# First queries and keys placed by 0/1 products, values projected by rows, and smaller first loads in a decoder kernel

## The reference

```python
# step 1: self attention, 8 sequences of 128 tokens, 8 heads of 8
qk = (x @ Wqk_w.T + Wqk_b).reshape(b, n, H, E, 2)
q, k = qk[..., 0], qk[..., 1]                      # (b, H, n, 8)
v = (x @ Wv_w.T + Wv_b).reshape(b, n, H, E)
attn = softmax(q @ k^T) / 8
x = layernorm(x + (attn @ v) @ Wo_w.T + Wo_b)
# step 2: cross attention of the context with x, softmax over 128 rows
x = layernorm(x + softmax(ctx @ x^T * 128**-0.5) @ ctx)
# step 3: linear layer with routed low-rank part
# step 4: 4-bit coded weights: attention products, gate, up, down
# step 5: cross attention with keys Wk, queries Wq and biases bq, bk
# step 6: gated feed-forward net with ternary weights
```

## Time and profile before

| | us |
|---|---|
| median of three runs | 661.75 (661.51 to 661.8) |
| the profiled execution | 661.55 |
| its span, first to last instruction | 659.7 |
| PE busy | 642.2 (97%), 3232 records |
| DVE busy | 394.1 (60%) |
| ACT busy | 384.2 (58%) |
| mean granted clock of PE | 0.996 |

### The profile page before, as it was taken

One profiled execution on the slowest core, in us unless ns is written; L12 is line 12 of the kernel. 1 busy time (PEld: TensorE's weight loads), 2 busy tenths in 40 slices (PEclk: granted clock), 3 DMA queues, 4 the chain that ended last, 5 costly groups with the idle time before them and its releaser, 6 DMA issues.

```text
span 659.7 us, 8518 instructions
## 1 busy us (share of the span) xinstructions
PE 642.2 (97%) x3232; PEld 473.7 (72%) x3232; DVE 394.1 (60%) x622; ACT 384.2 (58%) x528; POOL 67.5 (10%) x117
## 2 busy tenths in 40 slices
PE   9999999999999999999999999999999999999995
PEld 6655455554547778888888888886777888888874
DVE  2778867749688859676766527324675221215566
ACT  3877778866787777766767236213456333226532
POOL 1122213302231000000000000001111000000012
PEclk9999989999999999999999999999999999999999
DMA  6870287522323324332421003038000222100002
GB/s 226 294 269 33 85 267 192 160 80 64 100 99 108 103 70 141 102 108 77 126 79 31 1 0 129 1 113 365 0 5 29 80 97 67 61 1 0 1 32 97
DMA packets 25015, 64.19 MB, mean 97 GB/s; under 512 B 5478, under 2 KB 10022, under 8 KB 24079
## 3 DMA queue, kind: packets, MB, share of 16 engines
q1 hardware_dynamic: 23486, 61.50, 28.9%
q10 hardware_dynamic: 1488, 2.15, 1.0%
HBM read 58.90 MB, written 4.73 MB: 96 GB/s over the span
## 4 chain that ended last, share of the span: by engine, by line
PE 88%; DVE 4%; ACT 4%; issue 2%; POOL 1%; POOLq 0%; ACTq 0%; DVEq 0%
PE bank L1004 19%; PE bank L1083 8%; PE bank L1082 8%; PE bank L991 7%; PE bank L992 7%; PE bank L993 7%; PE bank L766 4%; PE bank L843 4%; PE bank L597 3%; PE bank L716 2%; PE bank L679 1%; PE bank L690 1%; PE bank L631 1%; PE bank L622 1%; PE bank L751 1%
## 5 line engine op out<-in xcount | busy, mean ns | idle before, releaser
L1191 ACT ACTIVATE line<-line 128x1024 f32<-128x1024 f32 x87 | 91.2, 1049 | 0.1
L991 PE MATMUL bank<-xh,wh 128*128 128x512 f32 x224 | 87.5, 391 | 0.0
L992 PE MATMUL bank<-xl,wh 128*128 128x512 f32 x224 | 87.4, 390 | 0.0
L993 PE MATMUL bank<-xh,wl 128*128 128x512 f32 x224 | 87.3, 390 | 0.0
L1004 PE MATMUL bank<-wh,xh 128*128 128x512 f32 x192 | 76.0, 396 | 0.2 <-DVE xl L2082 0.2
L1004 PE MATMUL bank<-wh,xl 128*128 128x512 f32 x192 | 74.9, 390 | 0.0
L2165 DVE SCALAR_TENSOR_TENSOR arena<-bank,ff_s,arena 128x512 f32<-128x512 f32 x28 | 21.0, 751 | 72.9 <-PE bank L1083 63.7
L2082 DVE TENSOR_TENSOR xl<-arena,xh 128x1024 fp32r<-128x1024 f32 (+1 forms) x26 | 29.6, 1141 | 35.2 <-ACT xh L1508 35.0
L1082 PE MATMUL bank<-xh,wh 128*128 128x512 f32 x128 | 50.2, 392 | 0.0
L1083 PE MATMUL bank<-xl,wh 128*128 128x512 f32 x128 | 49.9, 390 | 0.0
L1508 ACT ACTIVATE xh<-arena 128x1024 fp32r<-128x1024 f32 (+1 forms) x26 | 25.6, 991 | 41.3 <-PE bank L1004 34.8
(11 more groups left out here) (211 smaller groups left out, 1276.2 us busy)
## 6 DMA issues: line engine op xcount, KB each, us to landing
codes<-in_c_gu SPq DMA_DIRECT2D x14, 512.0 KB, 3.6
scales<-in_s_gu SPq DMA_DIRECT2D x28, 256.0 KB, 3.8
codes<-in_t_gu SPq DMA_DIRECT2D x8, 512.0 KB, 4.2
codes<-in_c_dn SPq DMA_DIRECT2D x7, 512.0 KB, 5.1
scales<-in_s_dn SPq DMA_DIRECT2D x14, 256.0 KB, 4.0
fold<-in_t_dn SPq DMA_DIRECT2D x1, 3584.0 KB, 16.6
scales<-in_t_gu SPq DMA_DIRECT2D x6, 512.0 KB, 3.7
x<-in_x SPq DMA_DIRECT2D x2, 1024.0 KB, 6.0
```

The source lines that it names most:

```text
L991: pe.matmul(dst, wh[:, s, c:c + P], xh[:, k, cols], start=(k == 0), stop=False)
L992: pe.matmul(dst, wh[:, s, c:c + P], xl[:, k, cols], start=False, stop=False)
L993: last = pe.matmul(dst, wl[:, s, c:c + P], xh[:, k, cols], start=False, stop=(k == KD - 1))
L1191: nc.scalar.activation(below(slot), below(slot), ACT.Prelu, bias=bias, scale=scale, alpha=alpha).then_inc(bent, 1)
```

## The change

1. **Placement.** Queries and keys of the first 256 tokens no longer go over DRAM. A table `places` of zeros and ones is made from the identity by DVE; PE multiplies it with the projected rows (`place_heads`, four products of 256 columns into banks 2 and 3), DVE copies the queries and ACT the keys (`keys_placed`) to their places. The other three quarters still go over DRAM. The constant row is now row 8 of each group of 32 instead of row 0.
2. **Values by rows.** `v_projection`, its ACT copy and the transposes `v_rows` are gone. `values(b)` multiplies the tokens (as weights) with Wv's 64 columns, four products per block, so that the result has tokens on partitions; DVE adds the bias while it copies (`v_out`). `keep_warm` is gone; `values(4)` to `values(7)` stand near its places.
3. **First loads.** The weights are split in a q/k part (256 KB) and a v part (128 KB); the first quarter of x transposed is split in two halves of 128 tokens (256 KB each). ACT's queue starts with three transfers ahead of its first instruction; the first 512 KB of x hold two blocks instead of four. The warm-up has four products instead of six.
4. **Order of the fillers.** `key_span` is moved by one: three key steps in t = 1, one in t = 7. Therefore the second key step of an iteration is the first of a group, and ACT's `key_group_out` is moved ahead of `heads_exp`. The decoding units run one iteration later in the loop (seven in place of eight) and the extra unit is put in step 4 of the second phase. `key_columns` is cut in four pieces, each ahead of one of the four products of `keys(0)`.

```diff
-WARM = 6
-PLAN = ([1] * NT, [2], [0] + [1] * NT, [1] * 3 + [2, 2] + [1] * 5)
+WARM = 4
+PLAN = ([0] + [1] * (NT - 1), [2], [0, 1, 1, 1, 2] + [1] * 4, [1] * 3 + [2, 2] + [1] * 5)
...
-    first = 2 + KD * (t - 2)
+    first = 3 + KD * (t - 2)
...
         @block.sync
-            sp.dma_start(qkvT, i["qkvT"]).then_inc(in_qk, 16)
+            sp.dma_start(qkT, i["qkT"]).then_inc(in_qk, 16)
+            sp.dma_start(xT[:, :, P:PC], i["xT"][:, :, P:PC]).then_inc(in_x0b, 16)
...
-            project_in(0)
             sp.dma_start(qk_b[:, :], i["qk_b"]).then_inc(in_pb, 16)
-            sp.dma_start(v_b[:, :], i["v_b"]).then_inc(in_pb, 16)
-            project_in(1)
-            sp.wait_ge(q_blank, 1)
-            sp.wait_ge(k_blank, 1)
-            rows_to_dram(0)
-            dram_to_heads(0)
+            sp.dma_start(wv, i["wv"]).then_inc(in_wv, 16)
+            sp.dma_start(v_b, i["v_b"].partition_broadcast(P)).then_inc(in_pb, 16)
+            project_in(2)
+            sp.dma_start(codes[:, 0, :], i["c_qkv"][0]).then_inc(in_codes[0], 16)
+            sp.dma_start(s_qkv[:, :], i["s_qkv"]).then_inc(in_sqkv, 16)
+            sp.wait_ge(blanked, 1)
             rows_to_dram(1)
...
+            def values(b):
+                if b == 0:
+                    pe.wait_ge(in_wv, 16)
+                elif b == 4:
+                    pe.wait_ge(v_ready, 1)
                 for k in range(KD):
+                    last = pe.matmul(bank[V_BANK][:, b % 4 * HA:(b % 4 + 1) * HA], xT[:, k, b * P:(b + 1) * P], wv[:, k, :], start=(k == 0), stop=(k == KD - 1))
...
+            def place_heads():
+                pe.wait_ge(blanked, 1)
+                pe.wait_ge(qk_ready, 1)
+                for w, dst in enumerate((q_place, k_place)):
+                    for g in range(HG):
+                        last = pe.matmul(dst[:, g * PC:(g + 1) * PC], places[:, HG * w + g, :], qk_st[:, 0:PC], start=True, stop=True)
+                    last.then_inc(place_ps, 1)
...
+            def key_columns(c):
+                if c == 0:
+                    pe.wait_ge(kw_ready, KD + 2)
+                for m in range(3 * c, min(3 * c + 3, 2 * KD)):
+                    n, e = divmod(m, KD)
+                    pe.matmul(bank[0][:, m:m + 1], folded[:, n, e * P:(e + 1) * P], picked[:, :], start=True, stop=True)
...
             def keys(n):
                 for c in range(KD):
+                    if n == 0:
+                        key_columns(c)
                     last = pe.matmul(turn_bank(n)[:, :], kq_w[:, c, e * P:(e + 1) * P], ctxT[:, g, c, :], start=(c == 0), stop=(c == KD - 1))
...
         @block.scalar
             for t in range(2, NT):
-                unit_bends(t, 0)
+                unit_bends(t - 1, 0)
                 x_T_out(t - 2)
+                key_group_out(t - 2)
                 heads_exp(t)
-                key_group_out(t - 2)
-                unit_bends(t, 1)
+                unit_bends(t - 1, 1)
                 norm_tail(t - 1)
...
         @block.vector
-            for t in range(NT):
+            for t in range(1, NT):
                 augment(t)
-                if t < 2:
+                if t == 1:
+                    unit_part(0, 0)
+                    v_out(1)
+                else:
+                    if t == 2:
+                        unit_part(1, 0)
+                    unit_part(t - 1, 1)
+                attention_norm(t - 1)
...
```

More of the change, by code:

```diff
@@ L634, in v_rows @@
[L634 to L644 removed]
+                for h in range(2) if n == 0 else (0,):
+                    size = P if n == 0 else PC
+                    if h:
+                        pe.wait_ge(in_x0b, 16)
+                    t = slice(n * PC + h * P, n * PC + h * P + size)
+                    for k in range(KD):
+                        last = pe.matmul(bank[QK_BANK[n]][:, h * P:h * P + size], qkT[:, k, :], xT[:, k, t], start=(k == 0), stop=(k == KD - 1))
@@ L777, in _ @@
             warm_up()
-            for n in range(2):
-                qk_projection(n)
-                v_projection(n)
-            qk_projection(2)
-            pe.wait_ge(ident_ready, 1)
-            v_rows(0)
-            scores(0)
-            v_projection(2)
-            max_rows(0)
+            qk_projection(0)
+            values(0)
+            values(1)
+            place_heads()
+            qk_projection(1)
+            scores(0)
+            values(2)
+            values(3)
+            pe.wait_ge(ident_ready, 1)
+            max_rows(0)
+            qk_projection(2)
+            scores_T(0)
             qk_projection(3)
-            scores_T(0)
-            v_projection(3)
             heads_out(0)
             scores(1)
-            keep_warm(6)
+            values(4)
+            values(5)
             for t in range(1, NT):
@@ L1878, in _ @@
             sims_prob(1)
-            unit_part(NT + 1, 1)
+            unit_part(NT, 1)
             for u in plan(2, 1):
```

191 lines of the change are left out of this document (86 added, 105 removed).

## The result

The changed kernel takes 668.24 us (median of 4 runs, 667.65 to 669.8) against 661.77 of the kernel before on the same chip: 1.0103 times as long, with a 95% interval of 1.0081 to 1.0124. It is slower by 1%, where 660.0 was predicted, and it lies above the predicted range. Ratios leave out any execution more than 1.5% above the fastest of its kernel, here one of 1660.4 among four of the kernel before; its other three took 661.51 to 661.8. The profiled execution took 668.24 with a span of 666.3, so 6.6 us more span than the 659.7 of before.

What follows compares the result with a forecast made beforehand. PE's stream was taken to bound the kernel. Terms -2.2 + 1.8 - 1.8 + 0.5 = -1.7 took the profiled 661.55 to 659.85; with the median 0.2 above, 660.0 us, range 657.9 to 662.2.

Steps and rivals of the forecast that it cites:

- Term 1: Opening, to block 2's row maxima: earlier first scores put PE ahead, -2.2 us (range -0.8 to -3.3).
- the opening stays at half clock: Rival for the opening: PE does less, clock stays at or falls to 1.2 GHz until about 13; 663.5 us, chance 0.12.
- Term 2: Loop: key copy ahead of the exponential delays head products 0.3 us in iterations 2 to 7, +1.8 us.
- the loop absorbs the copy: Rival for the loop: a gap or slack takes the key copy, cost 0 or near it; 658.2 us, chance 0.15.
- Term 3: Bias columns at keys(0): spread between large products, the half clock should not come, -1.8 us.
- the first rival: At keys(0): the clock falls all the same despite the spread columns; 661.8 us, chance 0.16.
- Term 4: Second phase: ACT's extra bends in step 4 make PE wait for prob before context(5), +0.5 us.

Runs made afterwards that it cites:

- e12: e9 with Wv ahead of the q/k bias, and x's third and fourth quarters and the codes held back until Wv landed: 659.5 us, ratio 0.9977.
- e3: Changed kernel with six products of zeros between the first projection and the first values: 664.83 us, ratio 1.0074.
- e0: Changed kernel unedited, measured again: 666.17 us, ratio 1.007.
- e4: Changed kernel with the key steps' order of before and the key group's copy behind the exponential again: 661.05 us, ratio 1.0017.
- e6: e5 with the key steps' order of before and the key copy behind the exponential again: 663.67 us, ratio 1.0031.
- e8: Changed kernel with keep_warm's 6 and 5 identity products put back ahead of values(4) and values(6): 666.65 us, ratio 1.0099.
- e10: e9 with keep_warm's identity products put back and a warm-up of six products: 662.27 us, ratio 1.0036.
- e1: Changed kernel with the q/k bias issued behind Wv and the value bias in SP's queue: 664.32 us, ratio 1.008.
- e5: Changed kernel with Wv and both biases moved to ACT's queue behind 256 KB of x, x's second quarter to SP's: 666.46 us, ratio 1.0114.
- e9: e6 with a semaphore for each bias and the q/k bias ahead of Wv in ACT's queue: 660.57 us, ratio 1.0013.
- e2: Changed kernel with x's second and fourth quarters issued only once the first half quarters are there: 664.26 us, ratio 1.0041.
- e11: Kernel before with only the new key-step order and the key copy ahead of the exponential: 666.25 us, ratio 1.0086.
- e7: Kernel before with only the bias columns spread between the four products of keys(0): 660.0 us, ratio 0.9985.
- e13: e12 with the extra decoding unit in the second phase's last step in place of step 4: 658.79 us, ratio 0.9973.

## Why the prediction was wrong

**Term 1, the opening: -2.2 predicted, +4.0 measured. This is the step that failed.** The sentence was "Values of two blocks wait for Wv, third in its queue, until about 7.0". Wv stands fourth there, behind the q/k bias, and the landing times were those of the kernel before, where two transfers followed one another on SP's queue and ACT issued its first at 5.45; in the changed kernel ACT's three, 1.25 MB, are issued from 0.73 on. Wv landed at 10.0. Two costs came with it: the values started 2.76 later than in e12, and the clock fell behind the wait, which took 1.74 at the values (3.47 to the placing, in e12 1.73) and 1.66 at the placing (3.45 to the next projection, in e12 1.79). Together they are the 6.16 by which the first scores differ. ACT's late first copy (its biases at 11.4) lay beside the values. The rival "the opening stays at half clock" described this, named the wait for Wv as a cause, and got a chance of 0.12; it priced 7 us at half clock with 3.5, and the clock was low from 10.05 until beyond 16, for 3.4; the wait of PE itself it did not price. That filling PE's wait keeps the clock up is shown by e3, for its profiled execution. It is not the length of the wait alone: the clock fell behind waits of 1.66 to 2.88 in six profiled executions (the changed kernel, e0, e4, e6, e8, e10), not behind 0.83 to 1.27 (e1, e5, e9), and not behind 3.14 in e2. All the rest of the walk was right: in e12, with Wv there in time, first scores stand at 12.63 (12.6 predicted), the row maxima of block 2 at 32.15 (32.1), and before them is the wait for DVE that made up the sum. So the mechanism and the size of the gain were right, and its condition, a load in time, was not met.

The Trainium skill ("DMA: Bandwidth & Descriptors", Anatomy of one DMA) gives a fit, for one transfer on the GpSimd path, of some 2.0 us plus the bytes at 436 GB/s, which for 128 KB is an estimate of 2.3 us. The traces here, on SP's and ACT's queues, show 7.5 with 1.25 MB beside it, 3.9 and 4.5 with less: in a loaded opening the fit does not give the landing, and the measurement decides.

**Term 2, the loop: +1.8 predicted, +2.4 measured.** The wait of PE was forecast at 0.5 and is 0.52. The period grew by 0.44 in the iteration shown and not by 0.3; interval by interval, from the maxima of block 2 to `sims(0)`, it is 0.65, 0.42, 0.44, 0.34, 0.24 and 0.29. Of the first, 0.2 is there in e12 too, with the order of before. The exponential starts 0.47 behind the key copy, and the key copy 0.50 behind the copy of the transposed block (42.06, 41.59, 41.09). Before, the exponential began 0.69 behind that copy, because it waited for the scores. So ACT's row moves by 0.28, as forecast. But the head products moved by 0.43, since PE's path is the longer one: the key step starts 1.24 behind the transposed scores, as forecast, and takes 1.06 where I had given it 0.9. In iteration 7 no key step is left in that place and PE waits 1.44 for the exponential, but the head products come only 0.29 later than before (2.16 behind the transposed scores, 1.87 before), the 0.3 of the forecast. e4 and e11 show the price of this part from both sides: 44.63 in place of 46.79 without it, and with it alone in the kernel before +2.2 over the same stretch. The rival "the loop absorbs the copy" did not happen.

**Term 3, the columns: -1.8 predicted, -0.5 measured here.** As an edit alone it does what was said: in e7 there is no fall at `keys(0)`, and no time in the upper of the two groups. In the changed kernel's profiled execution the fall came all the same, as the first rival had it, but not at the columns: it lies over `sims(0)` and the output projection, some 1 us behind the wait of 1.44 which term 2's edit makes. That wait does not explain it: e0, e1, e2, e3, e5 and e8 have it too, and none of their profiled executions has a fall there. With no fall the stretch takes 10.83 (e2, e12), 1.5 less than before, so the size was 0.3 too large and the rest is a fall whose cause is open.

**Term 4, the second phase: +0.5 predicted, +0.7 measured.** Taking the unit away from step 4 gives all of it back: 0.73 between e12 and e13, and 40.35 is the 40.36 of before. The place was named rightly: from `keys(5)` to `keys(6)` it took 6.35 in place of 5.62, with the transposes and `context(5)` between them late. Only 0.21 of it is recorded as a wait for `prob`, and the size was taken a little too small.

**What stays open.** Where the clock falls in an execution of the changed kernel, and why there, is only described: the opening, the stretch from about 25 to 43 us and the place behind the loop are seen up to 130 us. Behind that, seven profiled executions (e0, e1, e3, e5, e7, e10, e11) have one more fall between 198 and 214 us, which costs 0.4 to 0.5, by the time from the ranks to the end: 528.7 to 528.8 in place of 528.3. Nor was it tried whether the small rows of the q/k bias alone delay Wv (Wv ahead of it: 4.9 and 5.1 in e5 and e6, 6.8 in e1; behind it: 6.2 and 8.0 in e9 and e10, 6.3 to 7.5 in the kernels with SP's queue unedited).

## What to carry to other kernels

Work that is moved to the front of a kernel needs its operands there. Count what is under way in all queues at that time and in which place the needed transfer stands, and don't take the landing time of a lightly loaded queue: here 3 us of late weights, and the half clock behind them, turned a gain of 2.2 into a loss of 4.0. When a filler is moved so that it waits for an engine, price both paths behind it. A profile is one execution: where the single times spread, set the granted clock of the others beside it, and ask of a suspected cause whether other profiles have it without the effect. Try the parts of a change alone: two were gains (the columns, and the opening with its load in time), two were losses (the order of the fillers, the unit in step 4).

## What was not expected of the hardware

- A transfer of 0.5 KB in 4-byte rows took 7.2 us to land, and 8.4 were needed for 32 KB, with megabytes under way beside them; in e12 4.6 and 5.1, and 3.5 for the former in the kernel before.
- The clock was at its 1.2 GHz level with PE busy for 13.32 of 13.70 us in e1, from 25.2 on, with 16.00 of 16.00 us of work at full clock before it and a wait of no more than 0.38 between. The same is seen in e0 (29.6 to 43.3). The Trainium skill ("TensorE: Matmul & The Clock Gate", part 1, what's actually happening) says of the rise at the start of matmul work that its place varies from run to run. The traces agree: the sixteen records of the first projection (L625) took 2.94 in the changed kernel's profiled execution and 2.55 in e0, the same kernel, with no wait recorded among them. Falls move too: the second came at 85 in the former and at 30 in the latter.
- The kernel before has two groups of times by itself, 658.8 to 660.4 and 661.3 to 662.4; with the columns spread, twelve executions stayed below the upper one (659.39 to 660.95). Its profiled execution, 661.55, had the fall at `keys(0)`; none of the lower group was profiled, so that the groups differ by this fall is likely and not shown directly.
